# Expert rows in four planes: a token's four choices sorted by expert, and the last loads cut up by plane

## What is computed

```python
logits = h @ router_w.T                       # 16 experts
probs = jax.nn.softmax(logits)
top_vals, top_idx = jax.lax.top_k(probs, 4)   # 4 experts per token
top_vals = top_vals / jnp.maximum(top_vals.sum(-1, keepdims=True), 1e-09)
comb = zeros((N, E)).at[arange(N)[:, None], top_idx].add(top_vals)
y = einsum('eni,eih->enh', silu(g) * u, w_down)      # g, u: gate and up of each expert, width 176
routed = einsum('enh,ne->nh', y, comb)
shared = silu(h @ sh_gate) * (h @ sh_up) @ sh_down   # width 704
sg = sigmoid(h @ sh_gate_w)
return routed + sg * shared                   # added to x
```

## Time and profile before

| | |
|---|---|
| median of three runs | 421.17 us |
| profiled execution | 425.43 us |
| its span, first to last instruction | 423.4 us |
| TensorE busy | 91% |
| VectorE, ScalarE, GpSimd busy | 52%, 35%, 44% |
| mean granted TensorE clock | 0.96 |
| share of TensorE in the chain that ended last | 69% |

### The profile page before, as it was taken

The page is one execution under the profiler, slowest core; times in us unless marked ns, Lnnn a source line. Parts: engine busy times, 40 slices in busy tenths (PEclk is TensorE's granted clock), DMA queues, the critical chain, the costliest instruction groups (busy, mean ns, idle before and its releaser), DMA issues.

```text
span 423.4 us, 6202 instructions
## 1 busy us (share of the span) xinstructions
PE 385.0 (91%) x1984; PEld 329.0 (78%) x1984; DVE 222.1 (52%) x533; ACT 147.4 (35%) x304; POOL 188.4 (44%) x176
## 2 busy tenths in 40 slices
PE   3998869998999999999999999597987798999996
PEld 3877859887888888888687887496976687899884
DVE  6785555279522122112588775563554344755557
ACT  2643364344543443333445262141221212222140
POOL 0604743565154554333121177445565676444500
PEclk9889999999999999999989999797999979999999
DMA  6975353165433332101112686212222233111285
GB/s 213 372 257 170 87 172 125 62 200 203 152 125 124 125 123 67 64 33 37 37 39 68 167 186 195 82 46 77 79 86 84 91 88 83 68 63 64 84 313 188
DMA packets 22004, 51.89 MB, mean 123 GB/s; under 512 B 3878, under 2 KB 9510, under 8 KB 21670
## 3 DMA queue, kind: packets, MB, share of 16 engines
q1 hardware_dynamic: 16022, 35.24, 25.2%
q0 software_dynamic: 5952, 16.26, 12.6%
HBM read 38.12 MB, written 13.37 MB: 122 GB/s over the span
## 4 chain that ended last, share of the span: by engine, by line
PE 69%; DVE 9%; another core or an unknown queue 6%; issue 5%; DMA 4%; ACT 2%; POOL 2%; SPq 2%; POOLq 0%; DVEq 0%; ACTq 0%
PE gu L1500 10%; PE gu L1501 10%; PE gu L1502 10%; PE y L1884 8%; PE gu L1863 3%; PE gu L1859 3%; PE gu L1860 3%; PE y L1502 3%; PE y L1500 3%; PE y L1501 3%; DMA w_raw<-y_k 3%; PE gu L1526 2%; PE gu L1786 1%; PE gu L1808 1%
## 5 line engine op out<-in xcount | busy, mean ns | idle before, releaser
L591 POOL TENSOR_TENSOR w_lo<-w_raw,w_hi 128x768 fp32r<-128x768 f32 (+3 forms) x26 | 34.4, 1342 | 77.5 <-ACT w_hi L716 61.0
L681 POOL DMA_INDIRECT y_k<-w_raw,put x47 | 46.1, 981 | 45.3 <-DVE w_raw L1417 37.9
L1500 PE MATMUL gu<-act_hi,w_hi 128*128 128x512 f32 x132 | 54.2, 411 | 0.7 <-DVE hid L1023 0.7
L1501 PE MATMUL gu<-act_lo,w_hi 128*128 128x512 f32 x132 | 52.8, 400 | 0.0
L1023 DVE TENSOR_TENSOR hid<-silu,gu 128x512 f32<-128x512 f32 x24 | 16.5, 688 | 67.2 <-PE gu L1502 67.1
L1502 PE MATMUL gu<-act_hi,w_lo 128*128 128x512 f32 x124 | 49.3, 398 | 0.0
L944 ACT ACTIVATE silu<-gu 128x176 f32<-128x176 f32 x47 | 15.0, 318 | 88.9 <-PE gu L1863 60.2
L1859 PE MATMUL gu<-w_hi,xgT 128*128 x94 | 40.1, 427 | 2.6 <-ACT xgT L899 1.4
L1410 DVE TENSOR_TENSOR hid<-silu,gu 128x176 f32<-128x176 f32 x47 | 15.8, 335 | 39.2 <-ACT silu L944 28.8
L1884 PE MATMUL y<-w_dn,t_hidT 88*128 x96 | 28.4, 424 | 4.6 <-DVE w_raw L1417 4.5
L745 ACT ACTIVATE hid_hi<-hid 128x512 fp32r<-128x512 f32 x24 | 15.2, 632 | 47.4 <-DVE hid L1023 47.4
(11 more groups left out here) (325 smaller groups left out, 906.2 us busy)
## 6 DMA issues: line engine op xcount, KB each, us to landing
w_raw<-in_w_gu SPq DMA_DIRECT2D x16, 352.0 KB, 4.6
w_raw<-in_wc SPq DMA_DIRECT2D x8, 576.0 KB, 5.3
w_raw<-y_k SPq DMA_DIRECT2D x5, 512.0 KB, 5.5
w_hi_f<-in_w0s SPq DMA_DIRECT2D x6, 368.0 KB
y_k<-hid SPq DMA_DIRECT2D x1, 2048.0 KB, 13.1
w_dn<-in_w_dn SPq DMA_DIRECT2D x1, 1936.0 KB
w_raw<-in_ws SPq DMA_DIRECT2D x5, 384.0 KB, 3.1
w_hi_f<-y_k SPq DMA_DIRECT2D x6, 256.0 KB, 4.2
```

The source lines that it names most:

```text
L591: nc.gpsimd.tensor_tensor(w_lo[par][:, w], w_raw[par][:, w], w_hi[par][:, w].bitcast(F32), ALU.subtract).then_inc(split, 1)
L681: nc.gpsimd.indirect_dma_start(d["y_k"], bass.IndirectOffsetOnAxis(ap=put[:, i:i + 1], axis=0), t_out[j], None).then_inc(s_y[j], 16)
L1500: T.matmul(out, w[0], x[0], start=start, stop=False)
L1501: T.matmul(out, w[0], x[1], start=False, stop=False)
```

## The change

The four experts of a token are sorted by number before the masks are made: the numbers are negated, the other four columns hold -32, and a search for the eight largest brings the four numbers out in ascending order, which are negated again. Choice k of a token then always has an expert of number k or higher, and at most 12 + k. The weights can no longer be taken by rank of the logit; they are picked from the exponentials with the masks (a multiply of 128x512 and a reduction).

The row buffer is laid out in four planes of 1024 rows, one per choice; within a plane token t * 128 + p has row 8 * p + t. Since slot tiles are in order of expert, plane k is complete when tile 43 + k is written, whatever the routing. SyncE waits for that tile and loads the plane in two loads (tiles 0 to 3 and 4 to 7), of 128 partitions with four rows of 1 KB each, into buffers whose weights are no longer needed.

Tiles 5 to 7 no longer go over TensorE: ScalarE multiplies their loaded rows by the weight in place, GpSimd adds them. VectorE adds tiles 0 to 4 plane by plane, with the fourth late product between planes 0 and 1, and then the shared part of all eight tiles.

```diff
-ON_PE = 5
+ON_DVE = 5
...
-        late_f = w1_raw[:, 0:4 * HALF]
+        late_f = w1_raw[:, NT // 2 * H:NT // 2 * H + 4 * HALF]
...
-        y_in = [v.rearrange("p (k h) -> p k h", k=K1) for v in carve(w1_raw1, [K1 * H] * 5) + carve(w1_dn, [K1 * H] * 3)]
+        y_in_at = [[w1_dn[:, h * NT // 2 * H:(h + 1) * NT // 2 * H] for h in range(2)],
+                   [w[:, 0:NT // 2 * H] for w in (w1_hi_f, w1_raw)],
+                   [w[:, 0:NT // 2 * H] for w in (w1_hi1_f, w1_raw1)],
+                   [w1_dn[:, (2 + h) * NT // 2 * H:(3 + h) * NT // 2 * H] for h in range(2)]]
...
             # SyncE
-            for j in range(RING):
-                sp.wait_ge(s_y[j], Y_BEFORE[j] + 16 * len(range(j, SLOT_TILES, RING)))
+            for k in range(K1):
+                last_of_k = SLOT_TILES - K1 + k
+                for j in range(RING):
+                    sp.wait_ge(s_y[j], Y_BEFORE[j] + 16 * len(range(j, last_of_k + 1, RING)))
+                for h in range(2):
+                    t = slice(h * NT // 2, (h + 1) * NT // 2)
+                    sp.dma_start(y_in_at[k][h], d["y_k"][k * N:(k + 1) * N].rearrange("(p t) h -> p t h", p=P)[:, t]
+                                 ).then_inc(s_fin[2 * k + h], 16)
             for t in range(NT):
-                sp.dma_start(y_in[t], d["y_k"][0:N * K1].rearrange("(n k) h -> n k h", k=K1)[t * P:(t + 1) * P]
-                             ).then_inc(s_fin[t], 16)
-            for t in range(NT):
-                sp.wait_ge(s_fadd[t], K1 + 1 if t < ON_PE else 2)
+                sp.wait_ge(s_fadd[t], K1 + 1)
                 sp.dma_start(d["out"][t * P:(t + 1) * P], base(t)).then_inc(s_out, 16)
...
             # GpSimd, behind its last scatter
+            pool.wait_ge(s_bc, 2 * KH)
+            for k in range(K1):
+                for t in range(ON_DVE, NT):
+                    pool.wait_ge(s_wtd, k * (NT - ON_DVE) + t - ON_DVE + 1)
+                    if k:
+                        pool.wait_ge(s_fadd[t], k)
+                    nc.gpsimd.tensor_tensor(base(t), base(t), y_in(t, k), ALU.add).then_inc(s_fadd[t], 1)
...
             # ScalarE
-            act.wait_ge(t_dn, SLOT_TILES)
-            for t in range(ON_PE, NT):
-                for k in range(K1):
-                    A.activation(diag(t, k), cst[:, CS_ID:CS_ID + P], ACT.Copy, scale=r_w[:, t, k:k + 1]).then_inc(s_diag, 1)
+            for k in range(K1):
+                act.wait_ge(s_fin[2 * k + 1], 32)
+                for t in range(ON_DVE, NT):
+                    A.activation(y_in(t, k), y_in(t, k), ACT.Copy, scale=r_w[:, t, k:k + 1]).then_inc(s_wtd, 1)
...
             # VectorE, tables
+            V.memset(r_idf[:, :, K1:], -float(2 * E1))
...
-            chain(V.tensor_copy(r_idf[:], r_idx[:]))
+            chain(V.tensor_copy(r_idf[:, :, 0:K1], r_idx[:, :, 0:K1]))
+            chain(V.tensor_scalar(r_idf[:, :, 0:K1], r_idf[:, :, 0:K1], -1.0, None, ALU.mult))
+            for t in range(NT):
+                ins = V.max(r_ord[:, t, :], r_idf[:, t, :])
+            chain(ins)
+            chain(V.tensor_scalar(r_idf[:, :, 0:K1], r_ord[:, :, 0:K1], -1.0, None, ALU.mult))
...
-            V.tensor_tensor(r_lg[:, :, E1 + 1:], r_top[:, :, 0:K1], peak.broadcast_to([P, NT, K1]),
-                            ALU.subtract).then_inc(s_rlg, 1)
...
-            chain(V.tensor_tensor(r_w[:], r_ex[:, :, E1 + 1:], r_rec[:].unsqueeze(2).broadcast_to([P, NT, K1]), ALU.mult))
+            chain(V.tensor_tensor(r_oh[:], r_oh[:], r_ex[:, :, 0:E1].unsqueeze(1).broadcast_to([P, K1, NT, E1]), ALU.mult))
+            chain(V.reduce_sum(r_w[:].rearrange("p t k -> p k t"), r_oh[:], axis=AX_X))
+            chain(V.tensor_tensor(r_w[:], r_w[:], r_rec[:].unsqueeze(2).broadcast_to([P, NT, K1]), ALU.mult))
...
-            chain(V.scalar_tensor_tensor(out=y_row[:], in0=get[:], scalar=float(K1), in1=choice[:], op0=ALU.mult, op1=ALU.add))
+            V.tensor_scalar(y_p[:], get_i[:], P - 1, None, ALU.bitwise_and)
+            chain(V.tensor_scalar(y_t[:], get_i[:], P.bit_length() - 1, None, ALU.arith_shift_right))
+            chain(V.scalar_tensor_tensor(out=y_of_k[:], in0=choice[:], scalar=float(N - NT), in1=y_t[:], op0=ALU.mult, op1=ALU.add))
+            chain(V.scalar_tensor_tensor(out=y_row[:], in0=y_p[:], scalar=float(NT), in1=y_of_k[:], op0=ALU.mult, op1=ALU.add))
...
             # VectorE, tail
             def add_choice(t, k):
+                dve.wait_ge(s_fin[2 * k + t // (NT // 2)], 32)
                 if k:
                     dve.wait_ge(s_fadd[t], k)
-                else:
-                    dve.wait_ge(s_fin[t], 32)
...
-            for u in LATE:
+            for u in LATE[:3]:
                 late_product(u)
             dve.wait_ge(s_bc, 2 * KH)
-            add_choices(0, 2)
-            add_choices(2, 5)
+            add_choices(0)
+            late_product(LATE[3])
+            for k in range(1, K1):
+                add_choices(k)
             for t in range(NT):
                 add_shared(t)
-            for t in range(ON_PE, NT):
-                add_sum(t)
...
             # TensorE
-            for t in range(ON_PE, NT):
-                pe.wait_ge(s_diag, (t - ON_PE + 1) * K1)
-                pe.wait_ge(s_fin[t], 32)
-                for k in range(K1):
-                    ins = T.matmul(sum_ps[t - ON_PE][:, 0:H], diag(t, k), y_in[t][:, k], start=k == 0, stop=k == K1 - 1)
-                ins.then_inc(s_ysum, 1)
```

More of the change, by code:

```diff
@@ L217, in build @@
         r_idx = r_idx.bitcast(U32)
+        r_ord = r_choose[:, 0:NT * 8].rearrange("p (t e) -> p t e", t=NT)
         r_idf = sb("r_idf", [P, NT, 8])
@@ L248, in build @@
         y_row = sb("y_row", [P, SLOT_TILES])
+        y_of_k = sb("y_of_k", [P, SLOT_TILES])
+        y_p, y_t = (sb(name, [P, SLOT_TILES], I32) for name in ("y_p", "y_t"))
         get_i = sb("get_i", [P, SLOT_TILES], I32)
@@ L291, in base, with y_in @@
             return xT[:, b, s * HALF + at:s * HALF + at + n * H]
-        late_f = w1_raw[:, 0:4 * HALF]
+        late_f = w1_raw[:, NT // 2 * H:NT // 2 * H + 4 * HALF]
         late_silu = [silu[0][:], silu[1][:], late_f[:, 0:HALF], late_f[:, HALF:2 * HALF]]
         late_hid = [hid[0][:], hid[1][:], late_f[:, 2 * HALF:3 * HALF], late_f[:, 3 * HALF:]]
-        diags = w1_dn[:, 3 * K1 * H:3 * K1 * H + (NT - ON_PE) * K1 * P]
         own_cmp = xgT_f[0:1, 0:SLOT_TILES * E1].rearrange("p (i e) -> p i e", e=E1)
-        y_in = [v.rearrange("p (k h) -> p k h", k=K1) for v in carve(w1_raw1, [K1 * H] * 5) + carve(w1_dn, [K1 * H] * 3)]
+        y_in_at = [[w1_dn[:, h * NT // 2 * H:(h + 1) * NT // 2 * H] for h in range(2)],
+                   [w[:, 0:NT // 2 * H] for w in (w1_hi_f, w1_raw)],
+                   [w[:, 0:NT // 2 * H] for w in (w1_hi1_f, w1_raw1)],
+                   [w1_dn[:, (2 + h) * NT // 2 * H:(3 + h) * NT // 2 * H] for h in range(2)]]
+        y_in_at = [[v.rearrange("p (t h) -> p t h", h=H) for v in halves] for halves in y_in_at]
+        def y_in(t, k):
+            return y_in_at[k][t // (NT // 2)][:, t % (NT // 2)]
         def bank(name):
@@ L378, in build @@
         s_bd, s_ha = sem("cond_done"), sem("lora_down_done")
-        s_diag, s_ysum = sem("weights_on_diagonals"), sem("choices_summed")
+        s_wtd = sem("choices_weighted")
         s_own, s_ct = sem("experts_compared"), sem("slot_tables_ready")
@@ L916, in _ @@
             act.wait_ge(s_rlg, 2)
-            A.activation(r_ex[:], r_lg[:], ACT.Exp).then_inc(s_exp, 1)
+            A.activation(r_ex[:, :, 0:E1 + 1], r_lg[:, :, 0:E1 + 1], ACT.Exp).then_inc(s_exp, 1)
             shared(0, 1, lambda: turned(1))
@@ L1456, in add_choice, with add_choices @@
             def add_choice(t, k):
+                dve.wait_ge(s_fin[2 * k + t // (NT // 2)], 32)
                 if k:
                     dve.wait_ge(s_fadd[t], k)
-                else:
-                    dve.wait_ge(s_fin[t], 32)
-                V.scalar_tensor_tensor(out=base(t), in0=y_in[t][:, k], scalar=r_w[:, t, k:k + 1], in1=base(t),
+                V.scalar_tensor_tensor(out=base(t), in0=y_in(t, k), scalar=r_w[:, t, k:k + 1], in1=base(t),
                                        op0=ALU.mult, op1=ALU.add).then_inc(s_fadd[t], 1)
-            def add_choices(t0, t1):
-                for k in range(K1):
-                    for t in range(t0, t1):
-                        add_choice(t, k)
+            def add_choices(k):
+                for t in range(ON_DVE):
+                    add_choice(t, k)
             def add_shared(t):
@@ L1471, in add_shared @@
                 dve.wait_ge(s_d, 2 * (c + NC[SH]) - 1 + s)
-                if t < ON_PE:
-                    dve.wait_ge(s_fadd[t], K1)
+                dve.wait_ge(s_fadd[t], K1)
                 V.scalar_tensor_tensor(out=base(t), in0=Y[q // 2][s][:, (q % 2) * H:(q % 2 + 1) * H], scalar=sg[:, t:t + 1],
                                        in1=base(t), op0=ALU.mult, op1=ALU.add).then_inc(s_fadd[t], 1)
-            dve.wait_ge(t_hT, SLOT_TILES)
```

(14 more changed lines are left out.)

6 lines of the change are left out of this document (1 added, 5 removed).

## The result

The changed kernel takes 426.91 us (median of 20 runs), the kernel before 422.82 (20 runs): ratio 1.0103, 95% interval 1.0077 to 1.0129. The forecast was 2.0 us less; it came out 4.1 us more. The profiled execution took 427.53 us, with a span of 425.7 us against 423.4.

What follows compares the result with a forecast made beforehand. The tail bounds: scatter, 4 MB of loads, then VectorE. VectorE's end at 418.9 plus 2.5 gives 421.4 against 423.4, 2.0 us less, table work counted as nothing; from the median 419.2, range 415.4 to 423.0.

Steps and rivals of the forecast that it cites:

- Step 5: Tail, VectorE beside GpSimd: adds cost 0.55 us each (bounds 0.41 and 0.68), so VectorE ends at 418.9.
- step 1: Tail, loads: start 3.8 us earlier, 1.0 us given back to scatters; third landing at 407.4, eighth at 413.7.
- three signs of being wrong: Landings over 1.25 us apart, VectorE's last shared add waiting for GpSimd, or adds keeping their 0.41 us.
- Step 4: Tail, GpSimd: 12 new adds at 1.0 us each (bounds 0.744 and 1.36), ending at 418.5.
- The rival in which GpSimd becomes the bound: Tail, GpSimd's 12 adds set the end: at 1.36 us each, 2.3 us more than today; chance 0.13.
- third rival: Tail: early loads delay the last scatters, harmless up to 5 us, each us beyond costs one; chance 0.05.
- Step 2: Tail: diagonals go (24 matmuls, 12 copies, three sums); only VectorE's sums, 1.07 us, were on the path.
- Step 3: Tail, VectorE: still 20 adds, now plane by plane; late product delays nothing; plane 1 starts at 407.4.
- The table work: Between 215 and 250 us: sort (1.2 us) and weights hidden in VectorE's idle time; costs nothing, upper bound 1.2 us.
- The rival named this: Table work shows: TensorE waits 1 to 2 us for sort or weights, end at 422.4 to 423.4; chance 0.08.

Runs made afterwards that it cites:

- e6: The changed kernel with all 32 adds on VectorE, none on GpSimd and no scaled copies on ScalarE: 397.22 us, ratio to the kernel before 1.0086.
- e1: The changed kernel with tiles 5 to 7 summed on TensorE over diagonals, plane by plane, instead of GpSimd's adds: 395.43 us, ratio to before 1.0079.
- e4: The changed kernel without GpSimd's 12 adds (tiles 5 to 7 lack their experts' rows), ScalarE's copies kept: 394.55 us, ratio to before 1.0043.
- e3: The kernel before with only the sort and the pick of the weights added: 394.26 us, ratio to before 1.0046; run again, 1.0045.
- e9: The kernel before with the sort's instructions added on VectorE, their result unused: 394.41 us, ratio to before 1.0010.
- b2: The kernel before, unchanged, run again beside the changed kernel's variants: 394.25 us, ratio 0.9996.

## Why the prediction was wrong

**Step 5, the price of VectorE's adds, failed.** It took 0.55 us and bounded it by 0.68; measured are 0.87. The mechanism was named, the size came from a pair that bears it only in part: two VectorE subtractions of 128x512 slowed by 1.07 us in sum while a GpSimd subtraction began 0.22 us after them. Divided over both and halved for the smaller shape, this gave 0.27 us more. But each GpSimd add costs a VectorE add of 0.41 us another 0.46. If the 1.07 us are put down to the one GpSimd subtraction that ran in full beside the pair, half of it is 0.53, near the 0.46; this reading is not shown, but it would have been the upper bound to keep. The Trainium skill (SBUF — State Buffer, section "SBUF: two separate sides") calls the port pair that VectorE and GpSimd share an exclusive lock, for a VectorE instruction with two SBUF inputs beside a GpSimd one that reads SBUF: the later one is blocked for the other's whole instruction. The trace agrees that the two exclude each other, but not for the whole: with GpSimd's 0.76 us a pair would by that take an estimated 1.17, and it takes 0.87. The two engines together made no more adds than VectorE alone, as e6 shows. In the sum: the 15 adds of planes 1 to 3 took 10.9 us and not 8.3, 2.6 more. With the 1.4 us of step 1 that is the 4.0 us between the 418.9 forecast for VectorE's end and the 422.86 measured; the stores behind it took 0.3 us more. None of the three signs of being wrong named an add dearer than 0.55.

**Step 4** erred the other way: GpSimd's adds take 0.76 to 0.88, not 1.0. The rival in which GpSimd becomes the bound did not occur: its last add ends at 418.3, and VectorE does not wait for it.

**Step 1** was half right. The loads start 4.1 us earlier (3.8 forecast), but they did not flow at once at full pace: the DMA engines were busy for 74% from 399 to 402 and 91% from 402 to 405. So the third load, the first of plane 1, landed at 408.74 and not 407.4, and VectorE, which waited for it, began plane 1 at 408.76, 1.4 us late. And "plane 3's release stays at 403.0" failed: it came at 408.7. The eighth landing is at 415.04, where 413.7 was forecast. This is the third rival, given 0.05 and read as harmless up to 5 us and 1 us per us beyond. The scatter was 5.9 us later than unhindered, which at that price makes the landing 414.6; the price held within 0.4 us. The late landing did not reach the end, since VectorE was later still; in e1 and e4 it did. The Trainium skill (DMA: Bandwidth & Descriptors, section Queues, rings and completion order) has the DMA engines go round the queues packet by packet, which was taken to mean that scatters lose little. The runs show 2.6, 5.5 and 8.4 us with none, one and three planes sent before the scatter landed: it loses a great deal. In e1, without GpSimd, the step still brings 1.0 us of tail.

**Step 2** held: the three sums are gone from the end. **Step 3** held but for its start, above.

**The table work** was costed at nothing, since VectorE had 1.67 us of idle time before its product. Of the 1.2 us, 1.1 were there, but the idle time was not: it belongs to executions whose clock had fallen before it, and the changed kernel's profile, e3's and e9's have none. The logits shifted behind the sort are then late for ScalarE, and TensorE waits for it by 0.66 us. The cover was read in one execution, on VectorE's own queue, and not at those who wait for it. The rival named this, with chance 0.08 and 1 to 2 us; sorted order alone costs 0.45% by its ratio, which would be 1.9 us of 422.8. With the 2.5 us of tail it makes 4.4; 4.1 were measured. That the sum comes so close is no check: the 0.45% was measured on faster chips, and in the first comparison no run of the changed kernel has a clock above 0.970.

## What to carry to other kernels

Before work is moved to GpSimd beside VectorE instructions with two operands in SBUF, count what each GpSimd instruction adds to VectorE's: here 0.46 us for an add that VectorE makes in 0.41 by itself, so that 20 adds with GpSimd's help took VectorE longer than 32 without. A load sent ahead of a scatter's landing is not free: if a later step waits for that scatter, count its landing at two to three times what it takes alone. And idle time on the engine that gets new work hides it only if it is there in other executions too and nobody waits for what stands behind it; look at the granted clock of the stretch it was read in, and follow the results to the busiest engine.

## What had not been expected of the hardware

A scatter of 128 rows lands 2.4 us after its issue with no load beside it, and 8.1 us after it in e1, where three planes of 1 MB are sent before it lands. A fall of the granted clock to its lower level costs this kernel 2.2 us or more and comes in 17 of the 18 profiles at 207 to 222 or at 229 to 247 us, in two of them at both. The same kernel takes 393.6 us on one chip and 422.8 on another: on the slower the tile loop has waits without a named releaser (the earlier trace rows is one), and the stretch from 252 to 350 us, where TensorE is busy for 95.6 of 98 us in b2, has it busy for 83.1 in the kernel before, with a granted clock of 0.90 there against 1.00.
